# Four graph layers after an edge sort on one Trainium2 core: the weights prepared inside the sort, half of the high one-hots formed on GpSimd

## The reference

```
x = layernorm(x + L0(x))   # GATv2 attention, 4 heads, own edges added, summed by dst
x = layernorm(x + L1(x))   # attention from two scores per node, summed by src
x = layernorm(x + L2(x))   # 8-head dot attention, own edges added, softmax by row (src)
x = layernorm(x + L3(x))   # two relational layers: sum over edges of (h[src]+rel[etype]) @ Wn
```

## Time and profile before

| | us |
|---|---|
| median of 3 runs | 7950.01 (7939.81 to 7964.99) |
| the profiled execution, its own time | 7932.62 |
| its span | 7930.9 |
| constants, until 3.5 | 3.5 |
| load_weights with its barrier, 3.5 to 27.6 | 24.1 |
| loading and splitting of the edges, 27.6 to 41.9 | 14.3 |
| histograms, 41.9 to 270.9 | 229.0 |
| begins, own edges, run tables, 270.9 to 377.2 | 106.3 |
| places and scatters, 377.2 to 1407.9 | 1030.7 |
| the layers, from 1423 on | 6508 |

### The profile page before, as it was taken

The page is one execution under the profiler, slowest core; times in us unless marked ns, Lnnn a source line. Parts: engine busy times, 40 slices in busy tenths (PEclk is TensorE's granted clock), DMA queues, the critical chain, the costliest instruction groups (busy, mean ns, idle before and its releaser), DMA issues. The chain is left out here.

```text
span 7930.9 us, 112131 instructions
## 1 busy us (share of the span) xinstructions
PE 4807.8 (61%) x32954; PEld 3931.4 (50%) x32954; DVE 4479.6 (56%) x15028; ACT 2093.2 (26%) x4735; POOL 5513.5 (70%) x5311
## 2 busy tenths in 40 slices
PE   3699888566666647777756556554555556444442
PEld 2366665455655536666635555553444444333332
DVE  8999999577777653333346666665444443211113
ACT  8455444122222241111121111112232223111110
POOL 0377777577777557777747777774777774677775
PEclk9999999788888855555566777776555558555555
DMA  0022221566666436666546777762555553333333
GB/s 21 20 56 56 53 53 41 139 162 160 162 161 160 117 79 135 135 135 135 131 134 203 205 207 206 205 200 65 156 156 155 156 156 89 97 105 105 104 105 80
DMA packets 1304014, 990.39 MB, mean 125 GB/s; under 512 B 287713, under 2 KB 1192995, under 8 KB 1303411
## 3 DMA queue, kind: packets, MB, share of 16 engines
q0 software_dynamic: 183088, 352.33, 17.9%
q1 hardware_dynamic: 700995, 378.63, 17.1%
q10 hardware_dynamic: 419328, 252.26, 11.7%
HBM read 613.75 MB, written 368.79 MB: 124 GB/s over the span
## 5 line engine op out<-in xcount | busy, mean ns | idle before, releaser
L997 POOL DMA_INDIRECT l_rows<-tab,by_src x1664 | 1802.6, 1083 | 615.3 <-issue 506.6
L997 POOL DMA_INDIRECT l_rows<-tab,by_dst x832 | 976.3, 1173 | 324.0 <-issue 236.2
L997 POOL DMA_INDIRECT l3a_rows<-tab,by_dst x832 | 803.6, 966 | 297.7 <-issue 252.9
L997 POOL DMA_INDIRECT l3b_rows<-tab,by_dst x832 | 793.0, 953 | 294.4 <-issue 253.2
L715 POOL DMA_INDIRECT sorted_dst<-pay,place_i x783 | 792.2, 1012 | 275.3 <-issue 237.8
L1143 PE MATMUL l_ps_z<-l_win,l_sel_t 128*128 128x128 f32 x3328 | 747.2, 351 | 213.3 <-DMA l_rows<-tab,by_dst 187.0
L1444 PE MATMUL l3b_ps_o<-l3b_rows,l3b_sel 128*128 128x128 f32 x1664 | 425.7, 437 | 630.5 <-DMA l3b_rows<-tab,by_dst 630.5
L1143 PEld LDWEIGHTS l_ps_z<-l_win,l_sel_t 128*128 128x128 f32 x3328 | 601.6, 248 | 236.9 <-issue 183.1
L1444 PEld LDWEIGHTS l3b_ps_o<-l3b_rows,l3b_sel 128*128 128x128 f32 x1664 | 370.5, 328 | 686.0 <-issue 686.0
L1444 PE MATMUL l3a_ps_o<-l3a_rows,l3a_sel 128*128 128x128 f32 x1664 | 404.1, 419 | 480.2 <-DMA l3a_rows<-tab,by_dst 480.2
L1471 DVE TENSOR_SCALAR l3b_sel<-iota,by_dst 128x128 f32<-128x128 f16 x832 | 185.6, 302 | 859.4 <-PE l3b_ps_o L1444 855.9
(11 more groups left out here) (423 smaller groups left out, 12331.0 us busy)
## 6 DMA issues: line engine op xcount, KB each, us to landing
parts<-l_sums ACTq DMA_DIRECT2D x416, 264.0 KB
l_win<-win SPq DMA_DIRECT2D x1664, 64.0 KB
parts<-l3a_sums SPq DMA_DIRECT2D x208, 512.0 KB, 3.0
l_row<-slot_rows ACTq DMA_DIRECT2D x624, 128.0 KB, 3.2
parts<-l_sums ACTq DMA_DIRECT2D x208, 272.0 KB
parts<-l3b_sums SPq DMA_DIRECT2D x208, 256.0 KB
low_bc<-lo_rows SPq DMA_DIRECT2D x194, 256.0 KB
l_rows<-tab,by_src POOLq DMA_INDIRECT x1664
```

The costliest lines, as they stand in the source:

```text
L997: pool.indirect_dma_start(rows[:, q, g, :], None, table, bass.IndirectOffsetOnAxis(ap=index[:, k * G + g:k * G + g + 1], axis=0))\
```

## The change

1. `load_weights` is gone as a block of its own. Its tiles lie in tiles of the sort that are free by then (`ent`, `low`), and its work is spread over `sort_edges`: POOL's clears and SP's 27 DMAs stand behind the histograms (SP's behind the first four row fetches), the memset of `rel_w` at DVE's start, the rest of DVE's and PE's work behind the last unit's places, and SP's three piece moves in front of its wait for the scatters.
2. In the histograms DVE forms the high one-hots of the even units only. For odd units POOL forms them in two operations: it subtracts (tensor_tensor, 128x392), waits for itself, and compares with zero in place (tensor_single_scalar).
3. The low one-hots are shared 3 (DVE) to 5 (ACT) in even units, where it was 4 to 4, and 6 to 2 in odd units.

```diff
+        def whole(n):
+            return 6 if n % 2 else 3
 (PE)
                     pe.wait_ge(onehot, n + 1)
-                    for g in blocks(s)[:UD]:
+                    wait_count(pe, pool_hot, (n + 1) // 2)
+                    for g in blocks(s)[:whole(n)]:
 (ACT)
-                    for g in blocks(s)[UD:]:
+                    for g in blocks(s)[whole(n):]:
 (DVE)
-                        dve.tensor_single_scalar(lo[:, n % 4, g], wide[:, 0:P], low[:, k, at:at + 1], ALU.is_equal)
-                    high_hots(k, s, n % 4, onehot)
+                        ins = dve.tensor_single_scalar(lo[:, n % 4, g], wide[:, 0:P], low[:, k, at:at + 1],
+                                                       ALU.is_equal)
+                    if n % 2:
+                        ins.then_inc(onehot, 1)
+                    else:
+                        high_hots(k, s, n % 4, onehot)
...
+            dve.wait_ge(w_loaded, w_all)
+            dve.tensor_tensor(bias_rest[:, 0:D], bias_rest[:, 0:D], bias0, ALU.add).then_inc(w_split, 1)
...
 (POOL)
+            for i, k in enumerate(KEYS):
+                for s in range(US):
+                    u, n, at = i * US + s, len(blocks(s)), col(s, 0)
+                    if u % 2:
+                        wait_count(pool, counted, u - 3)
+                        pool.tensor_tensor(hi[:, u % 4, 0:n], replicate(high[:, k, at:at + n], 2, NT),
+                                           replicate(wide[:, 0:NT], 1, n), ALU.subtract).then_inc(pool_gap, 1)
+                        pool.wait_ge(pool_gap, u // 2 + 1)
+                        pool.tensor_single_scalar(hi[:, u % 4, 0:n], hi[:, u % 4, 0:n], 0.0, ALU.is_equal)\
+                            .then_inc(pool_hot, 1)
+            pool.memset(c.w1[:], 0.0).then_inc(w_cleared, 1)
+            pool.memset(c.one_rows[:], 1.0).then_inc(w_cleared, 1)
+            pool.wait_ge(counted, 2 * US)
+            pool.memset(zero_rows, 0.0).then_inc(w_cleared, 1)
 (SP)
+            sp.wait_ge(made, 8)
+            sp.wait_ge(counted, 2 * US)
+            sp.wait_ge(w_cleared, 3)
+            for to, of in loads:
+                sp.dma_start(to, of).then_inc(w_loaded, 16)
...
+            sp.wait_ge(w_split, 9)
+            for i in range(3):
+                sp.dma_start(c.bias_rows[i:i + 1, :], pieces[:, i]).then_inc(w_pieces_in, 16)
+            sp.wait_ge(w_pieces_in, 48)
             sp.wait_ge(self_sent, 16 * NT)
```

More of the change, by code:

```diff
@@ L135, in _, with sort_edges @@
             dve.tensor_copy(c.ident16[:], c.ident[:]).then_inc(cst_cast, 1)
-def sort_edges(nc, c, src, dst, etype, lo_rows, sorted_dst, runs, etype_at):
+def sort_edges(nc, c, w, src, dst, etype, lo_rows, sorted_dst, runs, etype_at):
     KEYS = (DST, SRC)
@@ L211, in sort_edges @@
         mult_done, split_done, shaped = kit.sem("sort_mult_done"), kit.sem("sort_split_done"), kit.sem("sort_shaped")
-        zeroed = kit.sem("sort_zeroed")
+        zeroed, pool_gap, pool_hot = (kit.sem(f"sort_{n}") for n in ("zeroed", "pool_gap", "pool_hot"))
+        w_cleared, w_loaded, w_turned, w_copied, w_split, w_pieces_in = (
+            kit.sem(f"w_{n}") for n in ("cleared", "loaded", "turned", "copied", "split", "pieces_in"))
+        rel_zero = kit.sem("w_rel_zero")
         stepped, steps_in, steps_out, rises_done, above_done = (
@@ L250, in _ @@
                 fetch(k, s)
+            sp.wait_ge(made, 8)
[3 more added lines that the diff above has]
+                sp.dma_start(to, of).then_inc(w_loaded, 16)
+            for table, width in pads:
+                sp.dma_start(table[NP:NW, :], zero_rows[:, 0:width]).then_inc(w_loaded, 16)
             for i, k in enumerate(KEYS):
@@ L284, in _ @@
                     pe.wait_ge(stepped, n + 1)
-                    for g in blocks(s)[UD:]:
+                    for g in blocks(s)[whole(n):]:
                         mm = pe.matmul(ps_step[i], lo[:, n % 4, g], hi[:, n % 4, g],
-                                       start=s == 0 and g == UD, stop=s == US - 1 and g == blocks(s)[-1])
+                                       start=s == 0 and g == whole(n), stop=s == US - 1 and g == blocks(s)[-1])
                     mm.then_inc(counted, 1)
@@ L411, in _ @@
                 permute((u - 5) // 2, (u - 1) % 2)
+            pe.wait_ge(w_loaded, w_all)
+            pe.wait_ge(mult_done, len(units))
+            pe.transpose(ps_t, c.w1[:, 0:D], c.ident[:]).then_inc(w_turned, 1)
+            for h in range(2):
+                mm = pe.transpose(ps_rt[:, h * (RELS // 2):(h + 1) * (RELS // 2)], rel_rows[:, h],
+                                  c.ident[0:RELS // 2, 0:RELS // 2])
+            mm.then_inc(w_turned, 1)
+            pe.wait_ge(w_copied, 1)
+            pe.matmul(ps_a, kernel_t, att_cols, start=True, stop=True).then_inc(w_turned, 1)
+            pe.wait_ge(w_copied, 2)
+            for h, (r0, r1) in enumerate(((0, P), (P, RELS))):
+                for l in range(2):
+                    mm = pe.matmul(ps_rw[0:r1 - r0, h, l], rel_t[:, r0:r1], c.w3[:, l, 0:D], start=True, stop=True)
+            mm.then_inc(w_turned, 1)
             pe.wait_ge(back_in, 16)
@@ L474, in _ @@
             dve.memset(zero_nt[:], 0.0).then_inc(prep, 1)
+            dve.memset(c.rel_w[:], 0.0).then_inc(rel_zero, 1)
             dve.wait_ge(filled, 6)
@@ L2035, in build @@
         constants(nc, c)
-        load_weights(nc, c, weights)
-        sort_edges(nc, c, src, dst, etype, lo_rows, sorted_dst, runs, etype_at)
+        sort_edges(nc, c, weights, src, dst, etype, lo_rows, sorted_dst, runs, etype_at)
         x_at = kit.sb("x_at", [P, NT, D])
```

145 lines of the change are left out of this document (52 added, 93 removed).

## The result

The changed kernel takes 7924.0 us (median of 14 runs, 7917.34 to 7937.48), the kernel before, timed beside it, 7942.35 us (14 runs, 7931.34 to 7964.99). The ratio is 0.9977 with a 95% interval of 0.9969 to 0.9985: 18 us less. That is a small gain, clear of noise by the interval, and inside the 0.3% (24 us) that the prediction counts as no change. The forecast was 7996 us and slower. The ratios are the recorded ones; they can differ from the quotient of the two medians by up to 0.001.

A forecast was written before the change was run, and what follows sets the result against it. In the histograms ACT was taken to end last, with DVE only 0.04 us per unit behind. Weights -24.1 us and DVE held by POOL +70 gave +46, 7996 us against the median; range 7890 to 8033.

The forecast's parts named there:

- DVE held by POOL: Histograms: POOL's pair holds DVE 1.1 us per two units, so the stretch grows from 229 to 299 us, +70; chance 0.52.
- rival 1: Histograms: no contention that counts, ACT stays the bound; -52.7 us, 7897; chance 0.34.
- Weights, -24.1 us: Start of the kernel: the weight block from 3.55 to 27.62 us goes and its work is hidden elsewhere, -24.1 us.
- The three covers: In the sort: moved work of POOL, SP (85 us of cover) and DVE (8.4 of 30 us) costs nothing.
- ACT's and DVE's own shares: Histograms, undisturbed: ACT needs 199.8 us and DVE 191, so ACT ends last and the stretch gives 28.6 us.
- POOL's pair: Histograms: POOL's subtraction and comparison together take 1.2 us, within 0.78 to 1.53.
- POOL by itself would keep up: Histograms: even 1.53 us per pair is under the 2.04 us that ACT's seven one-hots take.
- Nothing behind the histograms: Stages behind the histograms: the sum had no term for them beyond the hidden weight work, 0 us.
- sign of being wrong: Profile checks on the weights and histograms, such as a two-unit period of about 3.05 us and POOL's pair within 0.78 to 1.53.
- Rival 2: Histograms: each POOL operation costs DVE only 0.2 us, 39 in all, so only the weights' -24 remains, 7926; chance 0.14.

The follow-up runs named there:

- e1_again: Kernel before with only the weights moved into the sort, histograms as before: 7917.93 us, ratio 0.9974.
- x1_beside: Weights-only kernel plus unused POOL operations beside the histograms, by quarters none, subtraction, comparison, both: two units took 2.28, 2.84, 2.53, 3.05 us.
- p4_late: Weights-only kernel plus one unused POOL subtraction and comparison behind the sort's last scatter: ratio 1.0021 to the kernel before, on a 9185 us chip.
- e2b_pool: Kernel before with only the histogram part of the change, weights still a block of their own: 7947.04 us, ratio 1.0012.
- p1_pair: Weights-only kernel plus one unused POOL subtraction and comparison ahead of the histograms: 7885.18 us, ratio 0.9927 to the kernel before.
- p5b_before: Kernel before plus one unused POOL comparison, and the memset filling its tile, while edges load: 7907.17 us, ratio 0.9954.

## Why the prediction was wrong, step by step

The forecast was +46 us and the result -18, 64 us apart. Of these, 24 are the term for DVE held by POOL (+70, measured +46.6), and 40 come from the stages behind the histograms, which the sum took to be unchanged. That 7924 lies in the stated range all the same is luck: its low end was put there for the case of an undisturbed DVE (rival 1), and that is not what happened.

**Weights, -24.1 us: right.** The sort starts 24.05 us earlier, `e1_again` starts its scatters 24.4 us earlier and is 20.4 us faster. The three covers held: DVE's work ran from 1398.3 to 1407.0, 20.8 us ahead of the read back at 1427.86.

**ACT's and DVE's own shares: right as far as seen.** DVE's undisturbed steps are 0.163 and 0.48 us wherever the lows are read from SBUF, 1.95 us per two units; ACT has 51 us to spare.

**POOL's pair, taken 1.2 us and at most 1.53: wrong, 2.2 us.** The subtraction was put at the dear end, 0.77, and takes 0.85 by itself; the comparison was put at the cheap end, 0.39, and takes 1.24 to 1.34, 3.2 ns a column where the cast had 1.0. The cast was a bad neighbour, and the affine select (1.95 ns) closer but still too low. With it the sentence "POOL by itself would keep up" falls too: 98 pairs of 0.85 + 1.34 us are 215 us, more than ACT's 200, so by this estimate rival 1's 7897 could not be reached even without contention.

The Trainium skill ("GPSIMD Engine Reference", "Performance versus the Vector engine") has 2.6 cycles an element for a tensor_tensor, which the prediction turned into an estimate of 0.85 us. The subtraction agrees with it; the comparison has one input, and the figure isn't for it.

**DVE held for 1.1 us per pair, +70: the step that was mis-sized.** The direction was right, and rival 1 is false: DVE is the bound and everything else waits for it. It loses 0.86 us in two units, so 98 x (1.95 + 0.86) = 275 us, +46 and not +70. Two errors worked against each other: the pair is nearly twice as long as assumed, and DVE loses 0.6 us beside a subtraction of 0.93 to 1.1 and 0.25 beside a comparison of 1.2 to 1.5, not all of either. The assumption that POOL's operation holds DVE from first to last, since it reads and writes all the time, is what `x1_beside` refutes for the comparison. For the subtraction it is nearer the truth: DVE stands until the subtraction ends, but in the histograms not from its start, and in `p4_late` for all of it.

The Trainium skill ("SBUF — State Buffer", "Who interferes with whom") has the pair of ports held for the whole instruction. These runs agree with it on who is touched: tensor_scalar operations that read SBUF and the operation with two inputs there, but not the one that reads PSUM. They agree on the subtraction in so far as a low waits until its end (98.17 to 99.01), and not on the comparison, beside which lows go on. With the right size of this term the sum would have been -24 + 46 = +22, 7972: just inside the same by the 24 us bound.

**Nothing behind the histograms: wrong, and this decides the sign.** The sum ended with the two edited stretches, and no sign of being wrong looked behind them. In fact the histogram part wins 38 us behind itself (`e2b_pool`), the single pair 33 (`p1_pair`), the single comparison 41 (`p5b_before`). To get from -24 + 46 to the -18 measured takes -40, which lies within these. Rival 2 gave nearly this time (7926) for another reason: it had the histograms at +0. The records of the indirect DMAs on the pages shrink by 24.7 us, and the spans of the profiled executions win 24 (changed kernel), 31 (`e2b_pool` against before), 32 (`p1_pair` against `e1_again`) and 13 us (`p5b_before`) behind the first scatter. That timed runs give 33 to 41 may lie in the spread of single executions (some 15 us to either side), and no run divides it. Nor does a run show why one operation of POOL has this effect.

Could the split be mended? With 0.86 us lost whenever POOL takes a unit's highs, DVE with 8 lows of two units would need 8 x 0.163 + 0.48 + 0.86 = 2.64 us and ACT with 8 2.34; with 7 for DVE and 9 for ACT it would be 2.48 and 2.63. Both are over the 2.34 of before. This is worked out from the rows above and was not run.

## What to carry to other kernels

When a light engine is to take work from a bound one, measure first what its operation costs the bound engine while both run, by a scratch operation on data that nobody reads: one run with quarters gave each price apart. Such a price holds for the place where it was measured: in `p4_late` one operation of DVE lost 1.25 us beside the end of a scatter and a subtraction. Don't price an operation by another operation on the same engine. And when the traces differ by less than the edited stretches do, look at the mean duration of the instructions that were not edited, for the bound engine first: 5 ns on some 5000 instructions in series (24.7 us in the traces) outweighed the 22.9 us that the edited stretches had cost.

## What the runs showed of the hardware that was not expected

- GpSimd's indirect DMA instructions get some 7 to 10 ns shorter in the mean of the rows that little else disturbs (953 to 945 ns, 1012 to 1004 on the 7940 chips; 957 to 947 on the others) once GpSimd has run one subtraction or one comparison of tensors, and stay so to the end of the program. The kernel before runs memset, iota, cast and affine select on it, and these don't do it. Why is open; the runs show only that it needs to have run.
- GpSimd's comparison of an f16 tile with a number takes 1.19 to 1.66 us for 128x392 (1.34 with DVE idle), its subtraction of two tiles 0.85 with DVE idle and 0.93 to 1.12 beside it.
- In the histograms DVE lost 0.59 us beside a subtraction and 0.25 beside a comparison of GpSimd in operations that read from SBUF, and nothing in operations that read PSUM. Beside the subtraction the loss was one operation that ended with it; behind the last scatter one operation lost 1.25 us, beside the scatter's end and the whole of a subtraction.
- The same program takes 7940 us on some chips and 9185 on others, where GpSimd waits for DVE's places for 579 to 637 us and the shorter DMAs gave nothing.
